# Graph attention kernel: second attention pass respaced, TensorE's branch order turned round, c's ranks five tiles ahead of r's, absolute maximum in one VectorE step

## The reference, cut to what matters

```
# layer 0
deg = clip(adj.sum(1), 1);  dis = deg ** -0.5
diffusion = (dis[:, None] * adj * dis[None, :]) @ x - x
sim  = x @ x.T / (|x_i| |x_j|)
attn = softmax(beta * sim * adj, axis=1)
x = layernorm(x + diffusion + sigmoid(alpha) * (attn @ x - x))
# layer 1
XW = x @ W;  s_col = XW @ a[:f];  s_row = XW @ a[f:]
Z   = leaky_relu(s_row[:, None] + s_col[None, :], 0.01)
den = exp(Z);  num = adj @ den;  att = den / num (0 where num is 0)
x = layernorm(x + adj @ (att @ XW))
```

## Time and profile before

| | us |
|---|---|
| median of three executions | 649.95 |
| the profiled execution's own time | 648.9 |
| its span, first to last instruction | 647.1 |
| TensorE busy | 561.2 (87%) |
| VectorE busy | 496.8 (77%) |
| ScalarE busy | 419.7 (65%) |
| GpSimd busy | 403.8 (62%) |
| mean granted TensorE clock | 0.947 |

### The profile page before, as it was taken

The page is one execution under the profiler, slowest core; times in us unless marked ns, Lnnn a source line. Parts: engine busy times, 40 slices in busy tenths (PEclk is TensorE's granted clock), DMA queues, the critical chain, the costliest instruction groups (busy, mean ns, idle before and its releaser), DMA issues.

```text
span 647.1 us, 11836 instructions
## 1 busy us (share of the span) xinstructions
PE 561.2 (87%) x4145; PEld 346.3 (54%) x4145; DVE 496.8 (77%) x985; ACT 419.7 (65%) x713; POOL 403.8 (62%) x463
## 2 busy tenths in 40 slices
PE   0899999899898979997539898899999999969993
PEld 0555555343344868886538553444444444448882
DVE  3777877987996644788787867899998999985452
ACT  3888777699996614689966237787877888850000
POOL 6798887699998154556104235687777788204663
PEclk9899999999999689999558999999999999978997
DMA  7999985000000000000000121333332233000100
GB/s 128 107 109 108 108 298 189 1 1 1 2 0 7 1 8 24 21 18 10 18 1 26 54 81 48 95 95 90 90 101 64 81 104 95 24 5 18 29 26 17
DMA packets 19929, 37.23 MB, mean 58 GB/s; under 512 B 2586, under 2 KB 11054, under 8 KB 19854
## 3 DMA queue, kind: packets, MB, share of 16 engines
q0 software_dynamic: 7392, 24.32, 20.9%
q1 hardware_dynamic: 12462, 11.98, 5.6%
HBM read 48.72 MB, written 10.45 MB: 91 GB/s over the span
## 4 chain that ended last, share of the span: by engine, by line
PE 54%; DVE 21%; ACT 12%; issue 8%; POOL 1%; DVEq 1%; DMA 1%; SPq 1%; POOLq 0%; ACTq 0%
PE PSALL L1949 9%; PE PSALL L1573 8%; PE PSALL L1628 7%; PE PSALL L1641 6%; PE PSALL L1848 5%; DVE ring L1439 4%; DVE ring L1432 4%; PE PSALL L1777 3%; ACT AW L721 3%; PE PSALL L1908 3%; ACT ring L641 3%; PE PSALL L1618 2%; ACT PSALL L646 2%; PE PSALL L1609 2%; DVE FR L1439 2%
## 5 line engine op out<-in xcount | busy, mean ns | idle before, releaser
L444 POOL TENSOR_TENSOR R<-R,ring 128x452 f32<-128x452 f32 (+2 forms) x126 | 144.9, 1170 | 20.4 <-ACT ring L641 17.1
L1573 PE MATMUL PSALL<-XN 128*128 128x452 f16 (+2 forms) x396 | 97.8, 357 | 5.9 <-DVE ring L1022 5.8
L641 ACT ACTIVATE ring<-ring,sm 128x452 f32<-128x452 f32 (+1 forms) x132 | 86.9, 661 | 20.1 <-DVE ring L1022 19.8
L1848 PE MATMUL PSALL<-AW,R 128*128 128x452 fp8e4 (+1 forms) x348 | 77.5, 354 | 16.6 <-DVE R L1371 10.3
L1022 DVE TENSOR_TENSOR ring<-PSALL,AT 128x452 f32<-128x452 f32 (+1 forms) x132 | 81.0, 618 | 10.8 <-PE PSALL L1573 9.3
L505 POOL DMA_INDIRECT AW<-ATd,FR x44 | 56.1, 1276 | 32.5 <-DVE FR L1322 17.8
L1029 DVE TENSOR_TENSOR AW<-PSALL,ring 128x452 bf16<-128x452 f32 (+2 forms) x106 | 65.3, 617 | 8.4 <-ACT PSALL L646 8.1
L1908 PE MATMUL PSALL<-ring,XW 128*128 128x452 bf16 (+1 forms) x300 | 67.7, 360 | 1.0 <-DVE ring L1439 1.0
L1573 PEld LDWEIGHTS PSALL<-XN 128*128 128x128 f16 (+1 forms) x396 | 36.6, 97 | 53.7 <-DVE ring L1022 14.5
L646 ACT ACTIVATE PSALL<-ring 128x452 f32<-128x452 f32 (+2 forms) x106 | 58.4, 551 | 9.6
L1628 PE MATMUL PSALL<-ring,AO 128*128 128x452 bf16 (+2 forms) x220 | 62.3, 364 | 1.9 <-DVE AW L1029 1.7
(11 more groups left out here) (280 smaller groups left out, 1065.6 us busy)
## 6 DMA issues: line engine op xcount, KB each, us to landing
AT<-in_adjT POOLq DMA_DIRECT2D x22, 338.5 KB, 35.2
ATd<-AT SPq DMA_DIRECT2D x2, 3723.5 KB, 17.4
X<-in_x SPq DMA_DIRECT2D x2, 704.0 KB, 6.1
XWd<-ring SPq DMA_DIRECT2D x11, 128.0 KB, 1.8
out<-ring SPq DMA_DIRECT2D x21, 64.0 KB, 1.5
AW<-ATd,FR POOLq DMA_INDIRECT x44, 4.3
X<-XWd,idx POOLq DMA_INDIRECT x22, 2.5
Wt<-in_W SPq DMA_DIRECT2D x1, 64.0 KB, 3.2
```

Of the source, the lines that this page charges most:

```text
L444: i = G.tensor_tensor(ES_, ES_, z, ALU.add)
L641: S.activation(z, z, ACT.Exp, scale=bcol[0:rows, :]).then_inc(s_exp, 1)
L1573: m = TE.matmul(PSALL[0:rows, b, 0:w], lh[:, jt * P:jt * P + rows], rh[:, c0:c0 + w], start=(k == 0), stop=(k == 2))
L1848: TE.matmul(PSALL[:, b, 0:w], den_h[:, s + 1 + q, :, part], AW[:, jt % 3, q, c0:c0 + w], start=(q == 0 and part == 1), stop=False)
```

## The change

What it does, place by place:

- `roots` becomes five calls at five successive units. `scaled_rows` comes at every second unit from NH + 13 (u = 79 to 121), each `scaled_high` right behind the last row it needs (u = 90, 102, 114, 122), `scaled_low` three units behind it. `XD` was NH + 10, `HIGH` NH + 34, `LOWS` NH + 38.
- GpSimd's `sums_parts` of columns 3 to 5 and a memset move from behind the branch into it.
- TensorE's branch asks for flag 1 first; the turns stand inside both bodies, `spread(0)` behind the branch.
- The order of the rank steps: c's step t is paired with r's step t - 5. Four comparison buffers instead of three; the dump moves to other memory, for r from t = 15 on in the ring's. r's steps 12 and 13 come ahead of `settle(1)`, 14 behind c's `in_order`, 15 to 21 behind `w88`.
- `hots` comes behind `valued` and `places`.
- ScalarE's three `Abs` go; VectorE's reduction takes absolute values itself.

```diff
+        RL = 5
+        STEPS = [s for t in range(T - 5) for s in ((1, t), (0, t - RL)) if s[1] >= 0]
+        STEPS += [(1, t) for t in range(T - 5, T)] + [(0, t) for t in range(T - 5 - RL, T)]
...
+        def dump_late(kind, t):
+            return kind == 0 and t >= 15
+        def dump_of(kind, t):
+            return (RF if dump_late(kind, t) else FR)[:, 0:1408].bitcast(BF16)
...
-        ROOTS, XD, HIGH, LOWS = NH + 4, NH + 10, NH + 34, NH + 38
+        ROOTS, XD = NH + 4, NH + 13
+        HIGH = [XD + 2 * (t0 + nt) - 1 for t0, nt in SL]
+        LOWS = [u + 3 for u in HIGH]
... GpSimd
+                for c in range(HC, NC):
+                    sums_parts(c)
+                G.memset(AOT[:, N:NP], 0.0).then_inc(s_pad, 1)
...
-            for c in range(HC, NC):
-                sums_parts(c)
-            G.memset(AOT[:, N:NP], 0.0).then_inc(s_pad, 1)
... ScalarE
-                    if not shifted and 0 <= u - XD < T:
-                        scaled_rows(u - XD, 1)
+                    if not shifted and 0 <= u - XD < 2 * T and (u - XD) % 2 == 0:
+                        scaled_rows((u - XD) // 2, 1)
...
                 if it >= 6:
-                    for kind in range(2):
-                        row_sum(kind, it - 6)
+                    row_sum(1, it - 6)
+                    if it >= 6 + RL:
+                        row_sum(0, it - 6 - RL)
             xw_part("products", 9)
-            row_sum(0, 16)
+            row_sum(1, 16)
             xw_part("rows", 10)
-            row_sum(1, 16)
+            row_sum(0, 16 - RL)
             xw_part("products", 10)
             for t in range(T - 5, T):
                 row_sum(1, t)
-            for t in (T - 5, T - 4):
+            for t in (12, 13):
                 row_sum(0, t)
...
-            row_sum(0, T - 3)
+            row_sum(0, 14)
...
-            row_sum(0, T - 2)
-            row_sum(0, T - 1)
+            for t in range(15, T):
+                row_sum(0, t)
...
-            for p in range(3):
-                c0, w = wide_of(p)
-                av.wait_ge(s_YTd, 2 * p + 2)
-                S.activation(YA[:, c0:c0 + w], YT[:, c0:c0 + w], ACT.Abs).then_inc(s_yhi, 1)
... VectorE
-                    if u == ROOTS + 3:
-                        roots()
+                    if 0 <= u - ROOTS - 3 < 5:
+                        roots(u - ROOTS - 3)
...
-            rank_steps([(0, T - 4)])
+            rank_steps([(0, 13)])
             split_ok = thirds(1)
             settle(1)
-            hots(1)
             valued(1, split_ok)
             places(1)
-            rank_steps([(0, T - 3)])
+            hots(1)
...
+            rank_steps([(0, 14)])
...
-            rank_steps([(0, T - 2), (0, T - 1)])
+            rank_steps([(0, t) for t in range(15, T)])
...
-                    k = own.step(V.tensor_reduce(ln[:, p:p + 1], YA[:, c0:c0 + w], AX.X, ALU.max))
+                    k = own.step(V.tensor_reduce(ln[:, p:p + 1], YT[:, c0:c0 + w], AX.X, ALU.max, apply_absolute_value=True))
... TensorE
-            with eng.If(beta_large == 0):
-                attention(False)
+            with eng.If(beta_large == 1):
+                turns()
+                attention(True)
             pe.only(met)
             with eng.Else():
-                attention(True)
+                turns()
+                attention(False)
...
-            col_sums(0, T - 3)
...
+            for t in (14, 15):
+                col_sums(0, t)
             block_sums(0)
-            col_sums(0, T - 2)
-            col_sums(0, T - 1)
+            for t in (16, 17, 18):
+                col_sums(0, t)
             block_sums(1)
             both_parts(0)
+            for t in (19, 20, 21):
+                col_sums(0, t)
```

More of the change, by code:

```diff
@@ L653, in attention @@
                         copy_out(u - NH - 3)
-                    if not shifted and 0 <= u - XD < T:
-                        scaled_rows(u - XD, 1)
-                    if not shifted and 0 <= u - HIGH < 3 * len(SL) and (u - HIGH) % 3 == 0:
-                        scaled_high((u - HIGH) // 3)
+                    if not shifted and 0 <= u - XD < 2 * T and (u - XD) % 2 == 0:
+                        scaled_rows((u - XD) // 2, 1)
+                    if not shifted and u in HIGH:
+                        scaled_high(HIGH.index(u))
                 if shifted:
@@ L720, in row_sum @@
                 av.wait_ge(s_rowsum, m)
-                S.activation(Cb[3][0:rows, 0:(t + 1) * P], Cb[m % 3][0:rows, 0:(t + 1) * P], ACT.Copy,
+                if dump_late(kind, t):
+                    av.wait_ge(s_ends, 3)
+                S.activation(dump_of(kind, t)[0:rows, 0:(t + 1) * P], Cb[m % 4][0:rows, 0:(t + 1) * P], ACT.Copy,
                              accum_out=racc[kind][0:rows, t:t + 1]).then_inc(s_rowsum, 1)
@@ L970, in maxima, with roots @@
                 dv.wait_ge(s_maxz, 2 * NU + 3 * T)
[L972 to L984, removed]
+            def roots(n):
+                if n == 0:
+                    dv.wait_ge(s_dis, 3)
+                    dv.wait_ge(s_up, 1)
+                    own.step(V.tensor_tensor(cs, root0, root0, ALU.mult))
+                    return
+                dv.wait_ge(own.sem, own.n)
+                if n == 1:
+                    own.step(V.tensor_tensor(cs, cs, dis, ALU.mult))
+                elif n == 2:
+                    own.step(V.tensor_scalar(cs, cs, -0.5, 1.5, ALU.mult, ALU.add))
+                elif n == 3:
+                    own.step(V.tensor_tensor(dis, root0, cs, ALU.mult))
+                else:
+                    V.tensor_scalar(dup, dis, up_x, None, ALU.mult).then_inc(s_dis, 1)
             def scaled_low(k):
@@ L1033, in attention @@
                                             ALU.subtract).then_inc(s_low, 1)
-                    if u == ROOTS + 3:
-                        roots()
-                    if not shifted and 0 <= u - LOWS < 3 * len(SL) and (u - LOWS) % 3 == 0:
-                        scaled_low((u - LOWS) // 3)
+                    if 0 <= u - ROOTS - 3 < 5:
+                        roots(u - ROOTS - 3)
+                    if not shifted and u in LOWS:
+                        scaled_low(LOWS.index(u))
                 if shifted:
@@ L1116, in rank_steps @@
                     if t:
-                        V.tensor_scalar(Cb[n % 3][0:rows, 0:lo], key[0:rows, 0:lo], sc1, None, ALU.is_le).then_inc(s_less, 1)
-                    V.scalar_tensor_tensor(Cb[n % 3][0:rows, lo:lo + P], key[0:rows, lo:lo + P], sc1, U[0:rows, :],
+                        V.tensor_scalar(Cb[n % 4][0:rows, 0:lo], key[0:rows, 0:lo], sc1, None, ALU.is_le).then_inc(s_less, 1)
+                    V.scalar_tensor_tensor(Cb[n % 4][0:rows, lo:lo + P], key[0:rows, lo:lo + P], sc1, U[0:rows, :],
                                            ALU.is_le, ALU.mult).then_inc(s_less, 1)
@@ L1210, in _ @@
                 if it >= 5:
-                    rank_steps([(0, it - 5), (1, it - 5)])
+                    rank_steps([s for s in ((1, it - 5), (0, it - 5 - RL)) if s[1] >= 0])
             rank_steps([(1, t) for t in range(T - 5, T)])
@@ L1214, in _ @@
             V.memset(both, 0.0).then_inc(s_both, 1)
-            rank_steps([(0, T - 5)])
+            rank_steps([(0, 12)])
             dv.wait_ge(s_padr, 1)
@@ L1296, in _ @@
             settle(0)
-            hots(0)
             valued(0, split_ok)
             places(0)
+            hots(0)
             dv.wait_ge(s_dve, first_ok)
@@ L1556, in turn, with turns @@
                 m.then_inc(s_xnT, 1)
[L1558 to L1567, removed]
+            def turns():
+                turn(0)
+                turn(1)
+                pe.wait_ge(s_pm, 1)
+                TE.transpose(PSALL[0:1, 5, 0:P], pm, ident[:, :]).then_inc(s_scale, 1)
+                turn(2)
+                turn(3)
+                pe.wait_ge(s_top, 1)
+                TE.matmul(PSALL[:, 5, 0:1], orow, top, start=True, stop=True).then_inc(s_scale, 1)
+                turn(4)
+                turn(5)
             def logits(jt, c, b):
@@ L1697, in col_sums @@
                 for b in range(t + 1):
-                    ins = TE.matmul(PSALL[:, 6 - kind, b:b + 1], Cb[m % 3][0:rows, b * P:(b + 1) * P],
+                    ins = TE.matmul(PSALL[:, 6 - kind, b:b + 1], Cb[m % 4][0:rows, b * P:(b + 1) * P],
                                     ones[0:rows, :], start=False, stop=(t == T - 1 and b == t))
@@ L1722, in _ @@
                     pe.wait_ge(s_tail, TAIL * (it - 4) + 2)
-                if it:
-                    spread(it)
+                spread(it)
                 for g in (2 * it, 2 * it + 1):
@@ L1743, in _ @@
                 if it >= 7:
-                    for kind in range(2):
-                        col_sums(kind, it - 7)
+                    col_sums(1, it - 7)
+                    if it >= 7 + RL:
+                        col_sums(0, it - 7 - RL)
             xw_part("products", 9)
-            for kind in range(2):
-                col_sums(kind, 15)
```

(10 more changed lines are left out.)

15 lines of the change are left out of this document (6 added, 9 removed).

## The result

The changed kernel takes 666.53 us (median of 4 runs, 664.07 to 668.23), the kernel before 650.37 beside it on the same chip (four runs, 647.13 to 651.34): a ratio of 1.0257, 95% interval 1.0220 to 1.0293. The forecast was 653.4, with a range to 657.5. So the direction was that of the forecast (slower), the time lies outside its range, and the size was wrong by 13 us.

What follows compares the result with a forecast made beforehand. It took ScalarE to bound the second attention pass and r's late row sums, with other engines bounding other stages. Its terms summed to 3.4 us lost: 648.9 + 3.4 = 652.3 profiled, 653.4 against the median, range 644 to 657.5.

Steps and rivals of the forecast that it cites:

- Part 1: TensorE's choice at the start: a jump makes the first transpose late, 1.6 us lost; bounds 0 and -5.
- Rival C: At the start, between flag and first transpose: jump's fetch takes twice as long on loaded DMA engines, 656.8 us; chance 0.12.
- Part 7: End of the ranks: seven late row sums of r on ScalarE instead of two, 11.4 us lost.
- part 8: Behind r's last row sum: sums_out(0) and both_parts(0) hold up the column sums settle(0) needs, 3.2 us lost.
- Part 9: From settle(0) to L1178: VectorE's own starts set the pace, TensorE's block sums fit beside, 1.3 us won.
- Part 3: Attention's tail: GpSimd's sums start earlier and TensorE no longer jumps, 4.0 us won; bounds 2 and 5.
- Part 2: Second attention pass evened out: some of ScalarE's waits go, 2.0 us won; bounds 0 and +3.6.
- Parts 4, 5, 6, 9's own term, 10: Loop column sums +1.0; row sums until settle(1) +2.4; hots last +2.1; settle(0) to L1178 +1.3; one-step maximum 0.
- A: Ranks: the first half's gain lasts because r's late row sums are hidden or run at half price, 642.4 us; chance 0.13.
- B: A wash: start's jump hidden, second pass gives all 3.6 us, half clock costs nothing, about 650 us; chance 0.27.
- D: Second attention pass: evening out gains nothing, ScalarE's waits merely move, 655.4 us; chance 0.06.

Runs made afterwards that it cites:

- k2_oldchoice: The changed kernel with TensorE's choice as before (transposes ahead of the If, spread(0) inside): 658.57 us, 1.0157 of the kernel before.
- k9_quiet: k1_choice with GpSimd's adjacency loads held back until the transposes are done: 661.61 us, 1.0192 of the kernel before.
- k1_choice: The kernel before with only TensorE's choice turned round as in the change: 656.68 us, ratio 1.0137.
- k6_colfirst: The changed kernel with column sums t = 19 to 21 ahead of both_parts(0) on TensorE: 660.07 us, 1.0191 of the kernel before.
- k10_fill: The changed kernel plus 20 matmuls nobody reads in TensorE's idle time ahead of layer 1: 661.19 us, 1.0198 of the kernel before.
- k3_rl0: The changed kernel with r's ranks beside c's (lead 0 instead of 5): 652.29 us, 1.0045 of the kernel before.
- k7_rl0_old: The changed kernel with lead 0 for r's ranks and TensorE's choice as before: 645.84 us, 0.9955 of the kernel before.
- k8_best: k7_rl0_old with TensorE leaving its first body only behind spread(3) of the next loop: 646.68 us, 0.9953 of the kernel before.
- k11_pass2: The kernel before with only the second pass evened out and GpSimd's last sums inside its branch: 647.77 us, ratio 0.9992.
- k4_busy: The changed kernel with block_sums(3) computed twice in TensorE's idle time ahead of layer 1: 664.48 us, 1.0248 of the kernel before.
- k5_turns_ahead: The changed kernel with the 22 transposes ahead of TensorE's choice, which keeps its turned order: 665.39 us, 1.0250 of the kernel before.
- k12_best_fill: k8_best plus k10_fill's 20 matmuls in idle time ahead of layer 1: 643.93 us, 0.9930 of the kernel before.

## Why the prediction was wrong

**Part 1, the choice: the term that failed, by 7.4 us.** It took the price of a jump from the one row that had one, 2.85 us with a DMA share of 0.04 around it, and used it for a place where the share is 1.05. Flag to first transpose, less the 0.56 of reading: 6.6 us where the forecast had 2.85, so 5.37 late by itself, and a second standstill of 3.03 that the forecast didn't have (the last 0.6 of the 8.96 is about what k2_oldchoice shows without a jump). The bound of -5, worked out from one fetch of double length, was passed by the first standstill alone, and it left no room for a second. Rival C named the mechanism and the place, at 0.12, but its 3.4 us beyond the forecast were less than half of the 7.4. k9_quiet shows the mechanism in part: 5.4 us come with the load, 3.5 stay. The Trainium skill's rule that was quoted there ("Runtime: NRT & Kernel Launch", Instruction fetch mechanics: a taken branch to a page that isn't fetched waits for a DMA fetch) spoke against the part. It gives no price, and no trace here records a fetch; k1_choice and k9_quiet agree with it, as the same standstills are shorter when the DMA engines are quiet.

**Parts 7 and 8: right in mechanism.** Seven row sums in a row to 361.84, TensorE idle 6.50 (6.6 forecast). Part 7 measured -12.2 (c's ranks are in order 2.47 earlier, 334.40 against 336.87, and the last row sum ends 9.7 later; forecast -11.4), part 8 -3.8 (forecast -3.2; k6_colfirst takes out 3.8).

**Part 9 and layer 1: the second failure, 4.2 us.** "At half clock too (some 4 us to spare)" and the old distances from L1178 to the first product held (8.49 in both). What failed is that the sum had no term behind the first product, since nothing is changed there: the clock was at half in layer 1, where nothing covers it (k10_fill). The forecast had the half clock in its sum for one engine's stretch and not for the stretch behind the next idle time. But the longer idle time is only part of the cause. The distance from the first product to v = 2, by the idle time ahead of it:

| kernels | idle ahead | to v = 2 |
|---|---|---|
| the kernel before | 2.99 | 16.11 |
| k1_choice, k3_rl0, k7_rl0_old, k8_best, k9_quiet, k11_pass2 | 2.98 or 2.99 | 17.62 to 17.79 |
| k4_busy, k6_colfirst | 2.73, 3.11 | 17.64, 17.48 |
| the changed kernel, k2_oldchoice, k5_turns_ahead | 4.54 to 4.62 | 18.75 to 18.83 |
| k10_fill, k12_best_fill | 0.78, none | 16.11, 16.12 |

So about 1 us of the 2.64 goes with the longer idle time. The other 1.7 came in every version with the idle time of the kernel before, which alone escaped it; why it did is open. Behind v = 2 the changed kernel is 1.56 slower; there the versions scatter by 4.4 us (256.9 to 261.3 to the end), so no cause is shown for it beyond the 1.2 of v = 2's own half clock.

**Part 3: 2.95 where 4.0 was forecast.** No standstill and no half clock there, as forecast. 0.6 of the 4.0 falls behind this mark, on VectorE and ScalarE. Of the 3.4 for `row_sums`' 44 matmuls 2.7 came: GpSimd's sums ended 4.58 behind the start of the copy instead of 5.57, 1.0 won and not 1.47, and TensorE waited 1.19 for them.

**Part 2: right by luck.** -2.47 was measured and 2.0 forecast, but the edit gave 0.8 to 1.0; 1.5 goes with a half clock in the first pass, which the kernel before had and the changed one had not (k11_pass2, k1_choice). Evening out ScalarE's work won half of what the forecast took from its waits, or less.

**Parts 4, 5, 6, 9's own term, 10: right within about 0.5.** -3.91 for 4 and 5 (forecast -3.4, or -4.0 with the 0.6 of part 3), 2.1 for `hots` (`settle(1)` to c's order 8.45, was 10.55), -1.57 for 9. The maximum costs nothing: with absolute values the three reductions take the 3.07 us that they took without, and start 0.60 ahead of TensorE's transposes (0.33 in the earlier trace rows):

```profile
589.78 3.07 DVE L1502 TENSOR_REDUCE ln<-R 128x1 f32<-128x904 f32 x3
```

**Rivals.** A (gain lasts) decided on row sums at half price; they cost full price. B wanted a hidden jump; the reverse came. D asked for no gain from the evened pass; the pass was 2.47 shorter, though the edit's own share is 1.0 at most.

## What to carry to other kernels

Price a jump where it will stand, not where it stood: look at the DMA share of that stretch, allow for more than one standstill, and put the exit where the engine waits anyway. Work taken off a queue's front half comes back at its end, and what stands behind it in program order comes late too: before moving it, list what each engine has queued behind the last of it. Behind idle time of TensorE ahead of a bound stretch, new or old, allow for half clock, also where the profile before shows full clock: one trace of it is no promise. If the profile shows half clock, work without a reader in the idle time can be worth more than it costs. Before you credit an edit with a shorter stretch, compare the granted clock of both.

## What the runs showed of the hardware

- One far jump gave two standstills, with work between them: 4.84 and 3.03 us, 5.04 and 3.85, 6.59 and 4.16 under a full DMA load; 2.40 and 1.10 with quiet DMA engines.
- 20 matmuls that compute nothing made a kernel faster (k10_fill against the changed kernel, 1.0198 against 1.0257), with a granted clock of 1.00 instead of 0.50 in layer 1's first products.
- The kernel before ran layer 1's first products at full clock (1.69 us). Ten versions did not, all but the two with filling matmuls (1.92 to 3.17), though the idle time ahead was the same 2.98 or 2.99 us in six of them. To v = 2 the half clock costs 1.4 to 2.7 us.
- The same pass took 1.5 us more where some 3.4 us of its start ran at half clock (the kernel before against k1_choice).
- TensorE stood 0 to 1.55 us in the 22 transposes behind layer 1's If, in kernels that have the same code there.
